# A mixture-of-experts layer computed by dispatch: token rows sorted by expert, scattered to tiles of 128 slots and gathered back

## The chip, the cores and the metric

The kernel runs on one core of one Trainium2 chip. The metric is the time of one execution on the device in microseconds (us). The profile is of one further execution, recorded by the hardware. The engines are TensorE (PE; its weight loads are listed as PEld), VectorE (DVE), ScalarE (ACT), GpSimd (POOL) and SyncE (SP, which here issues most DMAs). Each engine runs its own program in order, and they wait for each other by semaphores. The core's 16 DMA engines are shared by the queues of SP, ACT and POOL.

## The reference, cut to what matters

There are 2 sequences of 1024 tokens of 128 features, all float32. Layer 0 is a causal attention of 16 heads and then the mixture of experts that is changed; layer 1 is a recurrence (RWKV) of 4 inner layers and a small mixture of 8 experts. Layer 1 needs all of layer 0's output of a sequence. The changed part is, with T = 2048 tokens, 64 experts of width 64 and one shared expert of width 128:

```
shared = silu(x @ sg_w.T) * (x @ su_w.T) @ sd_w.T
scores = sigmoid(x @ gate_w.T) + gate_bias           # [T, 64]
mask   = the 4 best of 8 groups of 8 experts
topk_w, topk_i = top_k(scores * mask, 6);  topk_w /= topk_w.sum() + 1e-8
comb   = zeros(T, 64) with topk_w at topk_i
h      = silu(einsum('th,eih->eti', x, eg_w)) * einsum('th,eih->eti', x, eu_w)
routed = einsum('eti,ehi,te->th', h, ed_w, comb)
out    = shared + routed
```

Each token has 6 of the 64 experts. The einsum over all experts is 64/6 times the work that the chosen ones need.

## The kernel before

The kernel holds activations transposed, features on the 128 partitions and tokens along the free axis: `G.x` is 128 x 2048, cut into 4 chunks of 512 tokens (`CH`, `NC` = 4; a chunk is one bank of PSUM). `stage_front` loads, normalises and projects; `stage_core` has the attention and the first layer's experts; `stage_rwkv` has all of layer 1.

The attention runs in 8 groups (4 heads of one sequence each) of 24 units. Scores go through banks 0 to 3, ACT takes their exponential, POOL masks the diagonal blocks, and TensorE multiplies with the values. Beside the units TensorE also computes the row maxima of the next group ("fills", banks 4, 5 and 7); they come back as rows through small DMAs (`neg_rows`, L598). In the last group the output projection, layer norm, router logits and routing (DVE) of chunks 0 to 2 run beside the units (`beside`, `last_group`).

The experts are dense. Step 0 is the shared expert, and steps 1 to 32 take two experts each, side by side in 128 hidden rows; so 33 steps of 4 chunks, 132 turns. A turn is three float32 matmuls of 128x128 weights on 512 columns (`gate`, `up`, `down`; L861, L866, L871), a Silu on ACT, and two multiplications on DVE (L1240, L1248), the second by the token's weight for that expert, which SP brings as broadcast rows (`factors`, L610) from a table in DRAM. `down` adds into 4 banks of PSUM over all steps. The loop over steps is rolled from step 6 on. At its end DVE adds the 4 banks times a gate to `G.x` (L1312), and `stage_rwkv` begins.

The order of work on each engine is written out by hand: `prologue` interleaves chunk 3's attention output and routing with the first steps, and `steps` runs the rest. SP loads weights two steps ahead, each load behind a wait for the last reader of its tile.

## Time and profile before

| What | Value |
|---|---|
| Time, median of 2 runs | 1076.97 us (1076.29 to 1077.66) |
| Span of the profiled execution | 1085.5 us |
| Attention's last matmul ends | about 322 us into the span |
| Last `down` of the experts ends | about 678 us |
| PE busy | 1016.3 us, 94% of the span |
| DVE, ACT, POOL busy | 767.1, 562.5, 63.4 us |
| Mean granted TensorE clock | 0.976 of full |

The span runs from the profiled execution's first to its last instruction; it is the only time that is known of that execution, and it is 8.5 us (0.8%) above the median of the unprofiled runs. Times in the rows are us from the start of the span, except where a column says ns.

### The profile page before, as it was taken

How to read it: one execution, taken by the hardware profiler on the slowest of the kernel's cores; microseconds unless marked ns; L12 is line 12 of the kernel's file. 1: busy time of each engine (PE TensorE's matmuls, PEld its weight loads, DVE VectorE, ACT ScalarE, POOL GpSimd, SP SyncE). 2: the span in 40 equal slices, each digit the busy share in tenths (PEclk: the TensorE clock that was granted, in tenths of full speed). 3: DMA queues.
4: the chain of work that ended last, by engine and by line, in shares of the span. 5: the costliest groups of instructions: out<-in, count | busy, mean ns of one | idle time of the engine just before them, and what ended most of it. 6: DMA issues, size and time to landing. Idle time of an engine off the chain costs nothing. (4 is left out here: it accounts for less than half of the span.)

```text
span 1085.5 us, 12065 instructions
## 1 busy us (share of the span) xinstructions
PE 1016.3 (94%) x3707; PEld 434.1 (40%) x3707; DVE 767.1 (71%) x1331; ACT 562.5 (52%) x854; POOL 63.4 (6%) x152
## 2 busy tenths in 40 slices
PE   6889999999888999999999999879999999998998
PEld 3553334444333344444444444324334433443433
DVE  4878788888466755555555555488889888987675
ACT  3324566666775222222222222567788768875743
POOL 1011122222210000000000000000000000000000
PEclk9899899999999999999999999889999999998999
DMA  2732122210021355555554552200000020000001
GB/s 84 230 78 49 37 55 56 55 48 12 7 60 46 84 134 126 109 133 120 113 134 112 119 133 50 63 1 0 10 22 8 3 51 0 1 0 1 1 1 39
DMA packets 36571, 64.66 MB, mean 60 GB/s; under 512 B 8514, under 2 KB 27824, under 8 KB 31920
## 3 DMA queue, kind: packets, MB, share of 16 engines
...
## 5 line engine op out<-in xcount | busy, mean ns | idle before, releaser
L1083 DVE TENSOR_REDUCE part_max<-psum 128x1 f32<-128x512 f32 (+3 forms) x304 | 184.6, 657 | 37.3 <-PE psum L723 21.4
L948 ACT ACTIVATE pt<-psum 128x1024 f32<-128x1024 f32 (+1 forms) x192 | 150.0, 814 | 112.5 <-PE psum L741 112.1
L1240 DVE TENSOR_TENSOR moe_gu<-moe_silu,psum 128x512 f32<-128x512 f32 x132 | 90.6, 687 | 141.4 <-PE psum L866 137.1
L1069 ACT ACTIVATE moe_silu<-psum 128x512 f32<-128x512 f32 x112 | 66.9, 597 | 222.1 <-PE psum L861 222.1
L861 PE MATMUL psum<-h,moe_wt 128*128 128x512 f32 x264 | 135.8, 596 | 1.0 <-issue 1.0
L866 PE MATMUL psum<-h,moe_wt 128*128 128x512 f32 x264 | 135.4, 594 | 1.4 <-DVE moe_gu L1240 1.4
L871 PE MATMUL psum<-moe_hid,moe_wt 128*128 128x512 f32 x264 | 135.3, 594 | 1.0 <-DVE moe_hid L1248 1.0
L719 PE MATMUL psum<-ka,qa 72*128 72x512 bf16 (+3 forms) x384 | 115.8, 342 | 4.5 <-DVE part_max L1083 1.6
L741 PE MATMUL psum<-qa,ka 75*128 75x512 bf16 (+3 forms) x384 | 95.3, 331 | 4.0 <-DMA qa<-neg_t 2.3
L1248 DVE TENSOR_TENSOR moe_hid<-moe_gu,qa 128x512 f32<-128x512 f32 x120 | 83.1, 692 | 15.7 <-DVE moe_gu L1240 5.8
L757 PE MATMUL psum<-pt,va_g 128*32 128x512 f32 (+3 forms) x768 | 82.9, 504 | 0.5 <-POOL pt L690 0.3
L871 PEld LDWEIGHTS psum<-moe_hid,moe_wt 128*128 128x128 f32 x264 | 50.3, 191 | 65.4 <-issue 63.6
L866 PEld LDWEIGHTS psum<-h,moe_wt 128*128 128x128 f32 x264 | 49.7, 190 | 66.4 <-issue 56.4
L861 PEld LDWEIGHTS psum<-h,moe_wt 128*128 128x128 f32 x264 | 50.2, 191 | 63.5 <-issue 63.5
L719 PEld LDWEIGHTS psum<-ka,qa 72*128 72x128 bf16 x384 | 37.6, 99 | 80.0 <-DVE part_max L1083 58.9
L690 POOL TENSOR_SCALAR_AFFINE_SELECT pt<-pt 128x256 f32<-128x256 f32 x128 | 52.3, 410 | 219.0 <-ACT pt L948 218.3
L1570 PE MATMUL psum<-mix_c,wt_c 128*128 128x512 f32 x128 | 61.1, 600 | 0.0
L83 PE MATMUL psum<-ln_sq,mean 128*128 128x512 f32 x88 | 49.5, 658 | 11.4 <-ACT ln_sq L92 11.4
L1580 PE MATMUL psum<-kf,wt_c 128*128 128x512 f32 x128 | 57.9, 594 | 0.0
L1527 PE MATMUL psum<-hp,wt_a 128*128 128x512 f32 x96 | 50.0, 603 | 2.7 <-issue 2.7
L723 PE MATMUL psum<-mask_qk,identb 128*128 128x128 bf16 x256 | 50.5, 226 | 0.0
L1528 PE MATMUL psum<-hp,wt_a 128*128 128x512 f32 x96 | 49.8, 600 | 0.0
(264 smaller groups left out, 1301.6 us busy)
## 6 DMA issues: line engine op xcount, KB each, us to landing
...
qa<-rows_q SPq DMA_DIRECT2D x21, 192.0 KB
ka<-rows_k SPq DMA_DIRECT2D x21, 192.0 KB
...
wt_c<-in_channel_w SPq DMA_DIRECT2D x4, 576.0 KB, 4.0
...
```

The costliest lines, as they stand in the source:

```text
L719: mm = pe.matmul(bank[:, nk * h:nk * (h + 1)], qa[0:ROWS, g % RING, h0 + h, chunk(i, P)], ka[0:ROWS, g % RING, h0 + h, k0:k0 + nk], start= ...
L741: mm = pe.matmul(out[:, 0:n], ka[0:ROWS + 3, g % RING, 2 * p + k, chunk(j, P)], qa[0:ROWS + 3, g % RING, 2 * p + k, q0:q0 + n], start=True ...
L757: mm = pe.matmul(acc_bank[32 * h:32 * h + 32, q0 - CH * c:CH], va_g[k][:, j, h, :], pt[:, 2 * (q % 2) + h // 2, h % 2, 0:n], start=(j == 0 ...
L861: pe.matmul(gate_bank(n)[:, :], weights[:, 0, :], G.h[:, chunk(c)], start=True, stop=True).then_inc(g_psum, 1)
L866: pe.matmul(u_bank[:, :], weights[:, 1, :], G.h[:, chunk(c)], start=True, stop=True).then_inc(u_psum, 1)
L871: pe.matmul(y_bank[c][:, :], weights[:, 2, :], hid[:, at, :], start=first, stop=last, skip_group_check=True).then_inc(y_psum, 1)
L948: act.activation(pt[:, u % 4, :, 0:n], score_bank[u % 2][:, :, 0:n], ACT.Exp, scale=SCALE)\
L1069: act.activation(sg[:, c % 2, :], g_bank[:, :], ACT.Silu).then_inc(silu_done, 1)
L1083: dve.tensor_reduce(part_max[:, h0:h0 + heads, slot], bank_of("fill", f)[:, 0:heads * nk].rearrange("p (h n) -> p h n", h=heads), AX_X, AL ...
L1240: dve.tensor_tensor(gu[:, at % 2, :], sg[:, at % 2, :], u_bank[:, :], ALU.mult).then_inc(gu_done, 1)
L1248: dve.tensor_tensor(hid[:, at, :], gu[:, at % 2, :], tile[:, chunk(c)], ALU.mult).then_inc(hid_done, 1)
L1570: pe.matmul(G.bank[6 + j % 2][:, :], wt_c[u // 2 % 2][:, WCK + j, :], mix_c[:, 0, q, :], start=True, stop=True)\
```

## The change

The dense loop is replaced by dispatch.

- Routing also keeps, per token and expert, whether it is chosen (`picked`). `positions(b)` counts the tokens of each expert of a sequence with matmuls, rounds each count up to a multiple of 128, and gives every (token, choice) a row in a table of slots; a tile of 128 slots has one expert. There are always 112 tiles per sequence, in 28 quads of 4 (`QUADS`), 56 quads in all, whatever the counts are; the table of one sequence is 14336 rows of 512 bytes.
- ACT's queue fills both tables with zeros during attention groups 1 to 4 (8 DMAs of 1.8 MB). The chunks of `h` are turned to token rows by TensorE. POOL scatters: 48 indirect DMAs per sequence, each of 128 rows of 512 bytes.
- The shared expert runs for 4 chunks between the attention and the quads (`shared`, `shared_down`).
- A quad is loaded by SP (256 KB), turned by 4 transposes, multiplied by its tiles' gate and up weights (4 matmuls of 128 columns), turned again after Silu and product, multiplied by the down weights (4 more), copied by ACT, and stored by SP (256 KB). The weights of all experts lie in SBUF (6 MB, in 4 parts, loaded during the last attention groups); their offset is read from SBUF into registers of TensorE (`pe.load`).
- POOL gathers 6 rows for each token (48 indirect DMAs per sequence), DVE weights and adds them (`combine`), TensorE turns the sums back, and DVE adds them to `G.x`.
- Semaphores of the first stage are cleared and freed, and those of layer 1's experts are made earlier.

The diff, cut to its core; `link` makes DVE wait for the instruction before:

```diff
+def load_experts(sp, G, A, k, sem):
+    few = slice(16 * k, 16 * (k + 1))
+    sp.dma_start(G.qa[:, k, :, :].rearrange("p h t -> p (h t)").bitcast(F32), A["moe_gu"][:, few, :].rearrange("p e m -> p (e m)"))\
+        .then_inc(sem, 16)
+    sp.dma_start(G.ka[0:64, k, :, :].rearrange("p h t -> p (h t)").bitcast(F32), A["moe_d"][:, few, :].rearrange("p e m -> p (e m)"))\
+        .then_inc(sem, 16)
...
+    QUADS = -(-((TOP * S - E) // P + E) // 4)
...
+        xs = pt[:, 0:2, :, :].rearrange("p u k n -> p (u k) n")
+        ys = pt[:, 2:4, :, :].rearrange("p u k n -> p (u k) n")
...
+                def weights(k):
+                    sp.wait_ge(score_psum, NU * (NG - RING + k + 1))
+                    load_experts(sp, G, A, k, experts_in)
+                def load_quad(n):
+                    if n >= 4:
+                        sp.wait_ge(xs_psum, n - 3)
+                    sp.dma_start(xs[:, n % 4, :], xs_d[n // QUADS].rearrange("(q p k) m -> q p (k m)", p=P, k=4)[n % QUADS])\
+                        .then_inc(xs_in[n % 4], 16)
+                def store_quad(n):
+                    sp.wait_ge(y_kept, n + 1)
+                    sp.dma_start(ys_d[n // QUADS].rearrange("(q p k) m -> q p (k m)", p=P, k=4)[n % QUADS], ys[:, n % 4, :])\
+                        .then_inc(ys_out[n % 4], 16)
 
...
                     neg_rows(g + 2)
                 pack(LAST - 1, 1)
+                weights(2)
                 pack(LAST, 0)
...
-                with sp.Fori(PRE // 2, (STEPS - 3) // 2) as i:
-                    for k in (1, 0):
-                        s = 2 * i + 2 - k
-                        sp.wait_ge(u_psum, 4 * s + 4)
-                        load_expert(sp, A, s + 2, wt[k], slice(0, 2), gu_in[k])
-                        sp.wait_ge(hid_done, 4 * s + 4)
-                        factors(s + 2, factor[1 - k], slice(0, T), factor_in[1 - k])
-                        sp.wait_ge(y_psum, 4 * s + 4)
-                        load_expert(sp, A, s + 2, wt[k], slice(2, 3), down_in[k])
+                weights(3)
+                for b in range(B):
+                    sp.wait_ge(scattered[b], 16 * INDEXED)
+                    sp.wait_ge(pv_done, NQ * NG)
+                    for q in range(4):
+                        load_quad(QUADS * b + q)
+                    for q in range(QUADS):
+                        store_quad(QUADS * b + q)
+                        if q + 4 < QUADS:
+                            load_quad(QUADS * b + q + 4)
...
+                def scatter(b):
+                    pool.wait_ge(zeroed[b], 16 * ZERO_PARTS)
+                    pool.wait_ge(h_kept, 2 * b + 2)
+                    pool.wait_ge(row_done, b + 1)
+                    for n in range(BLOCKS * b, BLOCKS * (b + 1)):
+                        for j in range(TOP):
+                            pool.indirect_dma_start(out=xs_d[b], out_offset=bass.IndirectOffsetOnAxis(ap=row[:, n, j:j + 1], axis=0),
+                                                    in_=h_tok[:, n, :], in_offset=None).then_inc(scattered[b], 16)
+                def gather(b):
+                    for r in range(4):
+                        pool.wait_ge(ys_out[r], 16 * (QUADS // 4) * (b + 1))
+                    for n in range(BLOCKS * b, BLOCKS * (b + 1)):
+                        if n >= 4:
+                            pool.wait_ge(combined, n - 3)
+                        for j in range(TOP):
+                            pool.indirect_dma_start(out=yg[:, n % 4, j, :], out_offset=None, in_=ys_d[b],
+                                                    in_offset=bass.IndirectOffsetOnAxis(ap=row[:, n, j:j + 1], axis=0))\
+                                .then_inc(gathered[n % 4], 16)
...
+                for b in range(B):
+                    scatter(b)
+                for b in range(B):
+                    gather(b)
...
+                def positions(b):
+                    pe.wait_ge(picked_done, 2 * b + 2)
+                    pe.wait_ge(const_done, 4)
+                    pe.wait_ge(prob_done, NU * NG)
+                    tiles = range(BLOCKS * b, BLOCKS * (b + 1))
+                    for n in tiles:
+                        mm = pe.matmul(count_bank[b][:, 0:E], all_ones[:, :], picked[:, n, :], start=(n == tiles[0]),
+                                       stop=(n == tiles[-1]))
+                    mm.then_inc(count_psum, 1)
+                    pe.matmul(rank_bank[b][:, :], earlier[:, :], picked[:, tiles[0]:tiles[-1] + 1, :].rearrange("p n e -> p (n e)"),
+                              start=True, stop=False, skip_group_check=True)
+                    for k in range(BLOCKS - 1):
+                        mm = pe.matmul(rank_bank[b][:, E * (k + 1):CH], all_ones[:, :],
+                                       picked[:, tiles[k]:tiles[k] + 1, :].to_broadcast([P, BLOCKS - 1 - k, E]),
+                                       start=False, stop=(k == BLOCKS - 2), skip_group_check=True)
+                    mm.then_inc(rank_psum, 1)
...
+                def turn_rows(n):
+                    pe.wait_ge(xs_in[n % 4], 16 * (n // 4 + 1))
+                    if n >= 2:
+                        pe.wait_ge(xs_kept, n - 1)
+                    for k in range(4):
+                        mm = pe.transpose(xs_bank[n % 2][:, chunk(k, P)], xs[:, n % 4, chunk(k, P)], G.ident[:, :])
+                    mm.then_inc(xs_psum, 1)
...
+                def gates(n):
+                    ids = at_expert[n % 4]
+                    pe.load(ids, expert_at[0:1, n // QUADS, 4 * (n % QUADS):4 * (n % QUADS) + 4])
+                    held[n] = [pe.snap(x, min_val=0, max_val=(E - 1) * P) for x in ids]
+                    pe.wait_ge(xs_kept, n + 1)
+                    if n >= 2:
+                        pe.wait_ge(hid_done, n - 1)
+                    for k in range(4):
+                        mm = pe.matmul(gu_bank[n % 2][:, chunk(k, P)], xs_t[:, n % 2, chunk(k, P)], gu_w[:, bass.ds(held[n][k], P)],
+                                       start=True, stop=True)
+                    mm.then_inc(gu_psum, 1)
+                def turn_hidden(n):
+                    pe.wait_ge(hid_done, n + 1)
+                    if n >= 2:
+                        pe.wait_ge(hid_kept, n - 1)
+                    for k in range(4):
+                        mm = pe.transpose(hid_bank[n % 2][0:64, chunk(k, P)], hid[:, n % 2, k, :], G.ident[:, :])
+                    mm.then_inc(hid_psum, 1)
+                def downs(n):
+                    pe.wait_ge(hid_kept, n + 1)
+                    if n >= 2:
+                        pe.wait_ge(y_kept, n - 1)
+                    for k in range(4):
+                        mm = pe.matmul(y_bank[n % 2][:, chunk(k, P)], hid_t[:, n % 2, chunk(k, P)], down_w[:, bass.ds(held[n][k], P)],
+                                       start=True, stop=True)
+                    mm.then_inc(y_psum, 1)
+                def turn_combined(c):
+                    pe.wait_ge(combined, 4 * c + 4)
+                    for t in range(4):
+                        mm = pe.transpose(comb_bank[c][:, chunk(t, P)], h_tok[:, 4 * c + t, :], G.ident[:, :])
                     mm.then_inc(comb_psum, 1)
...
+                def after_attention():
+                    positions(0)
+                    turn_h(2)
+                    turn_experts(0)
...
                     for c in range(NC):
...
+                        shared(c)
+                        shared_down(c)
+                def experts():
...
+                    for b in range(B):
+                        for step in range(QUADS + 3):
+                            n = QUADS * b + step
+                            if step < QUADS:
+                                turn_rows(n)
+                            if 1 <= step <= QUADS:
+                                gates(n - 1)
+                            if 2 <= step <= QUADS + 1:
+                                turn_hidden(n - 2)
+                            if step >= 3:
+                                downs(n - 3)
...
-                prologue()
-                steps(pe, step)
+                after_attention()
+                experts()
+                pe.wait_ge(xs_kept, NQUADS)
+                for c in range(NC):
+                    turn_combined(c)
...
+                def clear(part):
+                    b, k = part // ZERO_PARTS, part % ZERO_PARTS
+                    n = QUADS // ZERO_PARTS
+                    if part == 0:
+                        act.wait_ge(const_done, 1)
+                    act.dma_start(xs_d[b].rearrange("(q p k) m -> p q (k m)", p=P, k=4)[:, n * k:n * (k + 1), :],
+                                  zero[:, :].unsqueeze(1).to_broadcast([P, n, CH])).then_inc(zeroed[b], 16)
 
...
+                def keep_rows(n):
+                    act.wait_ge(xs_psum, n + 1)
+                    if n >= 2:
+                        act.wait_ge(gu_psum, n - 1)
+                    act.copy(xs_t[:, n % 2, :], xs_bank[n % 2][:, :]).then_inc(xs_kept, 1)
+                def silu(n):
+                    act.wait_ge(gu_psum, n + 1)
+                    if n >= 2:
+                        act.wait_ge(hid_done, n - 1)
+                    act.activation(sg[:, n % 2, :, :], gu_bank[n % 2][:, :].rearrange("p (k m) -> p k m", k=4)[:, :, 0:64], ACT.Silu)\
+                        .then_inc(silu_done, 1)
+                def keep_y(n):
+                    act.wait_ge(y_psum, n + 1)
+                    if n >= 4:
+                        act.wait_ge(ys_out[n % 4], 16 * (n // 4))
+                    act.copy(ys[:, n % 4, :], y_bank[n % 2][:, :]).then_inc(y_kept, 1)
+                def experts():
+                    for b in range(B):
+                        for step in range(QUADS + 3):
+                            n = QUADS * b + step
+                            if step < QUADS:
+                                keep_rows(n)
+                            if 1 <= step <= QUADS:
+                                silu(n - 1)
+                            if step >= 3:
+                                keep_y(n - 3)
...
+                def positions(b):
+                    at = slice(BLOCKS * b, BLOCKS * (b + 1))
+                    dve.wait_ge(count_psum, b + 1)
+                    link(dve.tensor_scalar(rounded[:, 0, :], count_bank[b][:, 0:E], P - 1.0, None, ALU.add))
+                    link(dve.tensor_scalar(rounded[:, 1, :], rounded[:, 0, :], 7, 7, ALU.arith_shift_right, ALU.arith_shift_left))
+                    link(dve.tensor_copy(sizes[:, :], rounded[:, 1, :]))
...
+                    link(dve.scalar_tensor_tensor(before_row[:, :], ends[:, :], 1.0, sizes[:, :], ALU.add, ALU.subtract))
+                    dve.wait_ge(rank_psum, b + 1)
+                    ins = dve.tensor_tensor(key[:, b, :, :], rank_bank[b][:, :].rearrange("p (n e) -> p n e", n=BLOCKS),
+                                            before_row[:, :].unsqueeze(1).to_broadcast([P, BLOCKS, E]), ALU.add)
+                    ins.then_inc(rank_read, 1)
+                    dve.wait_ge(rank_read, b + 1)
+                    link(dve.tensor_tensor(key[:, b, :, :], key[:, b, :, :], picked[:, at, :], ALU.mult))
+                    for n in range(BLOCKS):
+                        last = dve.max(top_key[:, BLOCKS * b + n, :], key[:, b, n, :])
+                    link(last)
...
+                    dve.tensor_tensor(row[:, at, :], row_part[:, 0, :, :], row_part[:, 1, :, :], ALU.bitwise_or).then_inc(row_done, 1)
...
+                def slot_weights(n):
+                    link(dve.tensor_tensor(same[:, :, :], key[:, n // BLOCKS, n % BLOCKS, :].unsqueeze(1).to_broadcast([P, TOP, E]),
+                                           top_key[:, n, 0:TOP].unsqueeze(2).to_broadcast([P, TOP, E]), ALU.is_equal))
+                    link(dve.tensor_tensor(same[:, :, :], same[:, :, :], chosen[:, n, :].unsqueeze(1).to_broadcast([P, TOP, E]), ALU.mult))
+                    link(dve.tensor_reduce(weight[:, n, :], same[:, :, :], AX_X, ALU.add))
...
+                def hidden(n):
                     dve.wait_ge(silu_done, n + 1)
...
+                    if n >= 2:
+                        dve.wait_ge(hid_psum, n - 1)
+                    dve.tensor_tensor(hid[:, n % 2, :, :], sg[:, n % 2, :, :],
+                                      gu_bank[n % 2][:, :].rearrange("p (k m) -> p k m", k=4)[:, :, 64:P], ALU.mult).then_inc(hid_done, 1)
+                def keep_hidden(n):
...
+                    dve.tensor_copy(hid_t[:, n % 2, :], hid_bank[n % 2][0:64, :]).then_inc(hid_kept, 1)
...
+                def combine(n):
+                    r = n % 4
+                    dve.wait_ge(scattered[n // BLOCKS], 16 * INDEXED)
+                    dve.wait_ge(gathered[r], 16 * TOP * (n // 4 + 1))
+                    dve.tensor_tensor(yg[:, r, :, :], yg[:, r, :, :], weight[:, n, :].unsqueeze(2).to_broadcast([P, TOP, P]), ALU.mult)\
+                        .then_inc(weighted, 1)
+                    dve.wait_ge(weighted, n + 1)
+                    dve.tensor_reduce(h_tok[:, n, :], yg[:, r, :, :].rearrange("p j m -> p m j"), AX_X, ALU.add).then_inc(combined, 1)
+                def add_experts(c):
+                    dve.wait_ge(comb_psum, c + 1)
+                    dve.scalar_tensor_tensor(G.x[:, chunk(c)], comb_bank[c][:, :], G.mod[:, 0, 5, c // 2:c // 2 + 1],
+                                             G.x[:, chunk(c)], ALU.mult, ALU.add).then_inc(G.x_l0, 1)
...
+                def experts():
+                    for b in range(B):
+                        for step in range(1, QUADS + 2):
+                            n = QUADS * b + step
+                            if step <= QUADS:
+                                hidden(n - 1)
+                            if step >= 2:
+                                keep_hidden(n - 2)
+                            if b and step % 3 == 0 and 0 < step // 3 <= BLOCKS:
+                                combine(step // 3 - 1)
+                    for n in range(BLOCKS, NT):
+                        combine(n)
+                    for c in range(NC):
+                        add_experts(c)
```


## Rows read from the trace of the kernel before

**Rows 1.** The page: busy time by engine, and TensorE's and the DMA engines' slices.

```profile
PE 1016.3 (94%) x3707; PEld 434.1 (40%) x3707; DVE 767.1 (71%) x1331; ACT 562.5 (52%) x854; POOL 63.4 (6%) x152
...
PEclk9899899999999999999999999889999999998999
DMA  2732122210021355555554552200000020000001
```

**Rows 2.** Windows: the end of attention, and the expert stage.

```profile
core 0: us, PE busy (x) PEld busy (x) DVE busy (x) ACT busy (x) POOL busy (x), PEclk, DMA share, GB/s
278.00:322.00 44.00, 36.37 (x238) 13.52 (x237) 24.54 (x95) 30.99 (x49) 9.33 (x23) 1.00 0.16 37
323.00:677.00 354.00, 347.92 (x813) 152.86 (x814) 198.28 (x347) 93.85 (x149) 0.00 (x0) 1.00 0.47 109
```

**Rows 3.** The page's costliest groups: the three matmuls of the expert loop.

```profile
L861 PE MATMUL psum<-h,moe_wt 128*128 128x512 f32 x264 | 135.8, 596 | 1.0 <-issue 1.0
L866 PE MATMUL psum<-h,moe_wt 128*128 128x512 f32 x264 | 135.4, 594 | 1.4 <-DVE moe_gu L1240 1.4
L871 PE MATMUL psum<-moe_hid,moe_wt 128*128 128x512 f32 x264 | 135.3, 594 | 1.0 <-DVE moe_hid L1248 1.0
```

**Rows 4.** Groups of DVE by line and shape: by number of columns.

```profile
L1248 DVE TENSOR_TENSOR moe_hid<-moe_gu,qa 128x512 f32<-128x512 f32 x120 | 83.1, 692 | 15.7 <-DVE moe_gu L1240 5.8 <-DMA qa<-comb_rows 2.1
...
L2157 DVE TENSOR_TENSOR den<-e,bb 128x1024 f32<-128x1024 f32 x8 | 9.7, 1216 | 0.0
...
L1191 DVE MAX8 best<-wide 128x8 f32<-128x64 f32 x16 | 2.4, 214 | 0.1
...
L1166 DVE TENSOR_TENSOR score<-score,gate_bias 128x256 f32<-128x256 f32 x4 | 1.7, 425 | 0.1
```

**Rows 5.** The 8 KB copies qa<-neg_t (L598): issue time, and landing.

```profile
L598 SPq DMA_DIRECT2D qa<-neg_t x27: 516/590/791, 54.4 to 280.6; - x27
...
DMA to landing us min/median/max: 1.8/1.9/3.7
```

**Rows 6.** Groups of TensorE by line and shape: small f32 matmuls and transposes.

```profile
L1677 PE MATMUL psum<-ident,x 128*128 128x128 f32 x16 | 2.6, 286 | 0.9 <-DVE x L2260 0.8
L794 PE MATMUL psum<-ident,chosen 128*64 128x128 f32 x16 | 2.5, 276 | 2.5 <-DVE chosen L1212 1.5 <-DVE h L1146 1.1
```

**Rows 7.** TensorE in order of time: 128-column matmuls at either clock.

```profile
25.20 1.05 PE L364 MATMUL psum<-wqkv,h_attn 128*128 128x128 f32 x8
26.09 0.60 PE L342 MATMUL psum<-ident,x_tok 128*128 128x128 f32 x4
...
56.37 3.13 PE L120 MATMUL psum<-ident,centre 128*128 128x128 f32 x16
59.34 0.60 PE L741 MATMUL psum<-qa,ka 75*128 75x512 bf16 x2
```

**Rows 8.** ScalarE's groups: the copy of one bank of PSUM.

```profile
L955 ACT COPY acc<-psum 128x512 f32<-128x512 f32 x16 | 9.5, 592 | 1.8 <-PE psum L757 1.7
```

**Rows 9.** The kernel's last stores (L1490, 256 KB each): time of the issue itself.

```profile
L1490 SPq DMA_DIRECT2D out_x<-v_s x2: 372/372/372, 1078.2 to 1082.8; - x2
```

**Rows 10.** DMA issues by tile: operation, count, KB each, median us from issue to landing.

```profile
wt_c<-in_channel_w SPq DMA_DIRECT2D x4, 576.0 KB, 4.0
...
raw_a<-in_time_w SPq DMA_DIRECT2D x4, 192.0 KB, 2.3
...
out_x<-k_s SPq DMA_DIRECT2D x2, 256.0 KB, 2.3
```

**Rows 11.** A register operation of SyncE in the old loop (L610).

```profile
L610 SPq FUSED_REGOPS  x52: 51/51/66, 398.5 to 656.7; - x52
```

**Rows 12.** TensorE in order of time: after an idle gap, in layer 1.

```profile
700.52 2.02 PE L1527 MATMUL psum<-hp,wt_a 128*128 128x512 f32 x2 [2.71 <-issue]
702.34 1.84 PE L1528 MATMUL psum<-hp,wt_a 128*128 128x512 f32 x2
...
719.80 3.24 PE L75 MATMUL psum<-r,centre 128*128 128x512 f32 x4 [3.61 <-DVE r L1342]
```

437 lines of the change are left out of this document (200 added, 237 removed).

## The prediction, made before the changed kernel was seen to run

> **What bounds the kernel now.** I read the page first: TensorE is busy 94% of the span and holds its full clock in nearly every slice [rows 1]. The windows then say what kind of busy it is. From 323 to 677 us TensorE works 347.9 of 354 us at clock 1.00, while DVE needs 198 and ACT 94 [rows 2]. The groups name the work: three lines of 264 records, together 406.5 us of busy time of which neighbours overlap a little [rows 3]. The expert stage lasts from the attention's last matmul at about 322 us to the last `down` at about 678, so 355 us, and is a pure TensorE stage. Everything that replaces it has to fit into those 355 us, whatever it saves in multiplications.
>
> **The span and the median.** The sum is made on the profiled span of 1085.5 us; I add its difference to the median of 1077 without scaling (0.8% of it is below what I can estimate).
>
> **Part 1, from the attention's end to the first quad.** `positions(0)` is on the path: 16 short bf16 matmuls, about 1 us, then on DVE two passes of 512 columns at 0.69 us, 8 MAX8 at some 0.15 us each (4 lines of them in a row, 214 ns alone), and about 12 linked small operations at 0.2 to 0.25 us [rows 4]: together 6.5 us. Then POOL issues 48 indirect DMAs, one after the other. No row shows one. Below it is bounded by an ordinary issue of SP, 0.5 to 0.6 us, and above by twice the whole round trip of a small copy, 1.9 us [rows 5], because 128 addresses have to be worked out by software. I take 1.25, the middle between issue and round trip, since issues need not wait for landings; so 48 x 1.25 = 60 us, plus 1.9 for the last to land and 2.6 for the first load. That makes 71 us. DVE has a chain of its own beside it: two `positions` (13), two chunks of routing (2 x 8), the shared expert in lockstep with TensorE and ACT (4 chunks of two matmuls on the path, 0.85 each, a Silu of 0.6, 0.69 and 0.75 on DVE: 3.8 each, 15), `slot_weights` of 16 blocks, each three operations on 384 columns (between 425 ns for 256 and 692 for 512, so 0.56 each [rows 4], 27 us in all), chunk 3's output and norm (6): 77 us before it can serve `hidden(0)`. So the phase takes 75 us, and scatters below 1.25 us would not shorten it.
>
> The Trainium skill weighs in here (DMA: Bandwidth & Descriptors, Anatomy of one DMA): a DMA from GpSimd has a fixed cost of about 2 us, most of which is completion latency, while descriptor generation is small. By that page successive issues could overlap and 48 of them would be nearer to the lower bound, so that the gather at the end would be some 30 us shorter; its section Rules for kernel authors (many small transfers are mostly overhead, coalesce them) speaks against the change. No row here shows which.
>
> **Part 2, one step of the quad loop.** TensorE's work in a step is 4 transposes, 4 matmuls, 4 transposes, 4 matmuls. Four float32 matmuls of 128 columns take 0.89 us from start to next start (25.20 to 26.09), and 4 transposes 0.60 to 0.65 with their tail, 0.5 without [rows 6, 7]. So 0.5 + 0.9 + 0.5 + 0.9 and a tail of 0.2 = 3.0 us at full clock. If this were all, 56 steps would be 168 us against 355. ACT's three operations (at most 0.59 each [rows 8]) and DVE's two (0.43 and at most 0.69 [rows 4], plus a third of a `combine` of 1.9) stay below that.
>
> But read SP's order. `load_quad(q + 4)` stands behind `store_quad(q)` in SP's queue, and `store_quad(q)` waits for `y_kept` of quad q. Quad q's `downs` is the last thing that TensorE does in step q + 3, and the first thing of step q + 4 is `turn_rows(q + 4)`, which waits for that very load. TensorE runs in order, so `gates`, `turn_hidden` and `downs` of the older quads wait behind it. The four buffers are thus worth nothing after the first four steps: every step is a closed ring. Its other half, after TensorE's last matmul: ACT copies y, 0.59 us [rows 8] and 0.05 of signalling; SP issues the store, 0.37 [rows 9]; the load lands. A 192 KB load takes 2.3 us, 576 KB takes 4.0 [rows 10], 4.4 ns per KB, so 256 KB is 2.6 alone. The 256 KB store that is 0.37 us ahead on the same 16 engines adds up to 1.13 - 0.37 = 0.76 if the two move one after the other, and nothing if they overlap; I take 3.1, between 2.6 and 3.4. Sum of this half: 0.65 + 0.37 + 3.1 = 4.1 us.
>
> Two more terms. `pe.load` reads 4 registers from SBUF between `turn_rows` and `gates`, in TensorE's own order. The trace has only register arithmetic, 51 ns [rows 11], as a lower end, and the 1.9 us round trip of the smallest copy as an upper one; a read of memory without a DMA lies between, and I take 0.8. The Trainium skill (DMA: Bandwidth & Descriptors, Latency and other measured facts) gives a floor of about 600 ns for `tensor_load`; by that the step would be 0.2 us shorter. And the clock: after idle gaps of 2.71 and 3.61 us TensorE runs its next matmuls at half clock (two records in 2.02 us where 1.02 is usual), for some 3 us [rows 12]. Here each step begins after 4 us of idling, so most of its work is at 1.2 GHz. The same small matmuls cost 1.65 times as much there: 16 records begin 2.97 us before the next (56.37 to 59.34) against 0.89 for 8, 1.78 for 16 [rows 7]. Fully slow the step's 3.0 would be 5.0; I take 1.3 of the 2.0, since the clock can come back within the step.
>
> The ring is then 3.0 + 1.3 + 0.8 + 4.1 = 9.2 us. It is paid in steps 4 to 27 of each sequence: 48 x 9.2 = 442 us. The first four steps of a sequence (10 us, with the inner waits of a pipeline that fills) and its three draining steps (6.5) make 33 us for both; the second sequence's first load again stands behind a last store, 4 us. Part 2 is 479 us.
>
> **Part 3, the tail.** After the last `y_kept` the store takes 0.65 + 2.3 us, and only then POOL gathers sequence 1: 48 x 1.25 = 60 us, 1.9 to land, a last `combine` of two operations on 768 columns (between 0.69 for 512 and 1.22 for 1024 [rows 4]), 1.9, 0.6 for the turn, 3.0 for `add_experts`, which the kernel before had too (0 here): 67 us. Sequence 0's gather lies beside sequence 1's quads, where DVE is idle most of the ring.
>
> **Part 4, beside the attention.** 14.7 MB of zeros at roughly 230 GB/s (from the 4.4 ns per KB) are 64 us of DMA time in groups 1 to 4, and DMA is only a fifth busy there [rows 1]. The row of neg copies that each group waits for is issued 5 units after a clear began; it may land up to a few us late: 0 to 12 us, I take 2. ACT issues 8 DMAs, hidden since ACT waits for TensorE in each unit. Clearing 23 semaphores behind a barrier: 1 us (0 to 3). The weights, 6 MB, come in the last groups; the fourth part lands behind the 71 us of part 1, and would cost about 7 us without that cover.
>
> **Sum.** New stage 75 + 479 + 67 = 621 us for 355: +266, and +3 from part 4: 1085.5 becomes 1354, and the median 1077 becomes about 1346.
>
> **The rivals.** (a) The ring as said, but the indirect DMAs dominate: at 2.5 us each the first phase is 131 us and the gather 120, together +116: 1462. For it speaks that software works out 128 addresses per DMA and no row caps it; against, nothing but the middle I chose. (b) The clock stays at 1.2 GHz through every step: the ring is 9.9 us, +34: about 1380. The Trainium skill's page (TensorE: Matmul & The Clock Gate, HAM oscillation) describes a loop whose DMA wait returns in each turn and which then starts cold every time; by that rule the time would be this one, and the trace agrees at the gaps of [rows 12] as far as single gaps can. (c) Clock full and loads quick (ring 7.2, indirect DMAs at 1.0): 75 + 346 + 37 + 55 = 513, so +158: about 1238. (d) The other side: the ring doesn't close, because a load lands before TensorE comes to `turn_rows`. Then the loop is bound by TensorE at 3.0 to 3.8 us, 56 x 3.4 = 190 us, and with 75 + 67 and 12 for draining and refilling it is 344, about 1069; with indirect DMAs at 0.6 us the tail shrinks by 31 us, to 1038, faster by 3.6%. It decides where the ring falls below (355 - 3 - 75 - 67 - 37) / 48 = 3.6 us, and speaking against it is the order of two lines in SP's queue: the wait for y can't be passed. (e) The stage doesn't shrink in columns as it says: 224 tiles of 128 slots are run always, 28672 rows for 12288; but that is in the sum.
>
> **How the numbers follow.** My forecast, the closed ring at 8 to 10.4 us with indirect DMAs of 1 to 1.8 us, spans 1275 to 1420 and has 0.62 (rival b's time lies in it, with 0.15 of that). Rival (a) has 0.15, rival (c) 0.15, rival (d) 0.04, and 0.04 is for what I haven't seen. The predicted time is that of the likeliest case, 1346. The range takes in (c) and reaches into (a) to 2.5 us per indirect DMA; left out are (d), the unseen and the slower half of (a), 0.16 in all: 1225 to 1470. About 2% is what a measurement of this kernel tells from no change; (d) splits around it: faster 0.03, same 0.02, slower 0.95.
>
> **What the changed profile would show.** TensorE's groups should be small ones and its busy share after 322 us below one half; the wait that heads its list should be the DMA into `pt` (xs) before `turn_rows`; starts of `turn_rows` should be 9.2 us apart after the fourth of a sequence and 3 to 4 us apart before; the granted clock between 0.5 and 1.0 in these windows. POOL's issues should be 1.25 us apart, 48 in a row, before the first quad and after the last. I am wrong in the main if TensorE waits for ACT or DVE in the loop instead, if steps are under 7 us, or if the POOL phases are longer than the ring's surplus.

## The result: 1441 us for 1077, and the profile of the changed kernel

The changed kernel takes 1440.96 us (median of two, 1437.92 to 1444.00) against 1076.97: the ratio is 1.338, with a 95% interval of 1.331 to 1.346. The profiled execution has a span of 1442.3 us, 356.8 more than the one before. It lies in the range I gave (1225 to 1470) and 95 us above the value. The page has these lines where [rows 1] stood:

```profile
PE 988.3 (69%) x4332; PEld 545.2 (38%) x4333; DVE 729.9 (51%) x1323; ACT 564.6 (39%) x888; POOL 249.6 (17%) x348
...
PEclk9899999995565555555755556565599999999999
DMA  4526551221210111111222211111100000100000
```

TensorE's busy time is hardly less than before. It runs fewer columns, but many of them at half clock: read PEclk, which is 5 or 6 tenths in nearly all slices from the tenth to the 29th. The windows, cut at the phases, are the answer to [rows 2]:

```profile
core 0: us, PE busy (x) PEld busy (x) DVE busy (x) ACT busy (x) POOL busy (x), PEclk, DMA share, GB/s
323.00:343.00 20.00, 9.02 (x18) 3.92 (x18) 14.21 (x61) 4.17 (x6) 15.43 (x16) 0.51 0.21 65
343.00:389.00 46.00, 3.57 (x18) 2.04 (x19) 9.63 (x49) 0.00 (x0) 35.03 (x37) 0.50 0.18 63
389.00:442.00 53.00, 18.68 (x24) 5.91 (x22) 5.77 (x9) 2.39 (x4) 40.20 (x43) 0.63 0.16 61
442.00:471.00 29.00, 6.93 (x28) 5.88 (x28) 26.66 (x49) 2.32 (x5) 3.04 (x3) 0.50 0.03 10
471.00:700.00 229.00, 137.82 (x625) 118.69 (x626) 29.41 (x55) 39.21 (x76) 0.00 (x0) 0.58 0.17 57
...
719.00:744.00 25.00, 0.19 (x2) 0.00 (x0) 3.42 (x4) 1.55 (x3) 14.26 (x15) 0.51 0.20 60
744.00:965.00 221.00, 133.30 (x615) 114.94 (x616) 43.89 (x65) 38.82 (x75) 21.86 (x24) 0.58 0.19 65
969.00:1032.00 63.00, 1.11 (x4) 0.71 (x4) 18.32 (x16) 0.00 (x0) 45.43 (x48) 0.50 0.18 50
```

Read them, with the start of layer 1 from the rows in order of time, as a sum from 316 us, where `positions(0)` begins, to 1037, where layer 1 begins: 155 us to the first `hidden(0)` at 471, 233 for the first sequence's quads, 262 for the second's, 71 for the tail, 721 in all. I had 75, 479 for both sequences, and 67.

The two long quad windows have TensorE at clock 0.58, idle 40% of the time. The groups name the wait:

```profile
L909 PE MATMUL psum<-ident,pt 128*128 128x128 f32 x224 | 61.4, 430 | 211.4 <-DMA pt<-slot_x 207.6 <-issue 3.8
...
L734 POOL DMA_INDIRECT slot_x<-va,slot_row x96 | 93.9, 979 | 36.4 <-issue 29.0 <-DVE slot_row L1371 7.5
...
L745 POOL DMA_INDIRECT part<-slot_y,slot_row x96 | 91.3, 951 | 491.8 <-DMA slot_y<-pt 398.8 <-DVE va L1442 65.6 <-issue 27.4
```

L909 is `turn_rows`, and its wait is the DMA into the quad's tile. One turn of the ring in order of time (weight loads left out):

```profile
578.02 0.32 SPq L668 DMA_DIRECT2D slot_y<-pt  x1
578.38 0.43 SPq L663 DMA_DIRECT2D pt<-slot_x  x1
581.08 1.12 PE L909 MATMUL psum<-ident,pt 128*128 128x128 f32 x4 [3.71 <-DMA pt<-slot_x]
581.99 1.92 PE L923 MATMUL psum<-qa,xs_t 128*128 x8
...
583.70 1.06 PE L932 MATMUL psum<-ident,moe_hid 128*64 128x128 f32 x4
...
584.69 2.07 PE L940 MATMUL psum<-ka,moe_hid_t 64*128 x8
...
586.80 0.58 ACT L1192 COPY pt<-psum 128x512 f32<-128x512 f32 x1 [2.47 <-PE psum L940]
587.41 0.32 SPq L668 DMA_DIRECT2D slot_y<-pt  x1
587.77 0.43 SPq L663 DMA_DIRECT2D pt<-slot_x  x1
```

From store to store 9.39 us, of which the copy of y, the store's issue and the load are 3.8. This is the ring of the prediction. About one step in three is a shorter one, of 8.3 to 8.5 us: there the clock comes back before the step's end, and the same `downs` takes 1.16 us, as in this line from 10 us earlier:

```profile
576.22 1.16 PE L940 MATMUL psum<-ka,moe_hid_t 64*128 x8
```

What the prediction did not have is the length of the first phase, and the hole of 25 us at 719. In the first phase the rows of DVE (the second routing and the shared expert, beside the scatter) look like this:

```profile
359.42 0.29 DVE L1355 TENSOR_TENSOR_SCAN ends<-all_one,sizes 128x64 f32<-128x64 f32 x1
360.61 0.23 DVE L1356 SCALAR_TENSOR_TENSOR before_row<-ends,sizes 128x64 f32<-128x64 f32 x1 [0.90 <-DVE ends L1355]
371.91 0.69 DVE L1358 TENSOR_TENSOR slot_key<-psum,before_row 128x512 f32<-128x512 f32 x1 [11.08 <-remote]
...
402.74 0.69 DVE L1414 TENSOR_TENSOR o_den<-o_den,psum 128x512 f32<-128x512 f32 x1 [8.13 <-remote]
408.27 0.75 DVE L1418 SCALAR_TENSOR_TENSOR x<-psum,mod,x 128x512 f32<-128x512 f32 x1 [4.84 <-remote]
```

L1358 waits for TensorE's ranking matmuls, which ended at 357.5, and for L1356 on its own engine, which ended at 360.8; it starts at 371.9. L1356 waits only for the instruction before it on its own engine, and starts 0.9 us after it. Operations that wait for nothing, such as 8 MAX8 in a row, run at their usual pace. That speaks against slow work or a contended port: what seems late is the moment at which an engine sees what it waits for, and the profile often knows no releaser for it (`remote`, `issue`). The delays begin 20 us after GpSimd's first indirect DMA (322.75), and its last is at 444.4.

Who waits for whom matters. One chunk of the shared expert, from the same stretch:

```profile
405.35 1.91 PE L893 MATMUL psum<-h,shared_w 128*128 128x512 f32 x2
...
413.91 0.60 ACT L1173 ACTIVATE o_den<-psum 128x512 f32<-128x512 f32 x1 [16.24 <-remote]
418.88 0.69 DVE L1414 TENSOR_TENSOR o_den<-o_den,psum 128x512 f32<-128x512 f32 x1 [9.86 <-remote]
419.62 2.07 PE L902 MATMUL psum<-o_den,shared_w 128*128 128x512 f32 x2 [10.71 <-DVE o_den L1414]
```

ACT starts 6.7 us after the matmul whose result it takes, and DVE, which waits for ACT and for a second matmul (over at 408.9), 4.4 us after ACT's end. TensorE starts 0.05 us after DVE's end. So it is in all the rows of these stretches: the long delays stand before operations of ACT and DVE that wait for TensorE. TensorE behind DVE or ACT, SyncE behind ACT and DVE's `hidden` behind ACT's Silu start 0.02 to 0.14 us later, with few exceptions, the longest 1.3 us. Late instructions, rather than late signals, would fit this pattern less well, but no run tells the two apart.

### The profile page after: what moved, and what is told of

Read it like the earlier page. It is cut to its first block and busy times, and to the rows that moved or that the text cites. A ratio compares the mean times of both kernels' runs of the same rounds, so it can differ in the third digit from the quotient of the medians.

```text
span 1442.3 us, 13431 instructions
## 1 busy us (share of the span) xinstructions
PE 988.3 (69%) x4332; PEld 545.2 (38%) x4333; DVE 729.9 (51%) x1323; ACT 564.6 (39%) x888; POOL 249.6 (17%) x348
## 3 DMA queue, kind: packets, MB, share of 16 engines
q0 software_dynamic: 6144, 12.60, 2.6%
## 5 line engine op out<-in xcount | busy, mean ns | idle before, releaser
L909 PE MATMUL psum<-ident,pt 128*128 128x128 f32 x224 | 61.4, 430 | 211.4 <-DMA pt<-slot_x 207.6
L745 POOL DMA_INDIRECT part<-slot_y,slot_row x96 | 91.3, 951 | 491.8 <-DMA slot_y<-pt 398.8
L1179 ACT COPY xs_t<-psum 128x512 f32<-128x512 f32 x56 | 32.8, 585 | 257.0 <-PE psum L909 219.6
L909 PEld LDWEIGHTS psum<-ident,pt 128*128 128x128 f32 x224 | 40.4, 216 | 225.4 <-DMA pt<-slot_x 220.0
L923 PE MATMUL psum<-qa,xs_t 128*128 x448 | 107.4, 420 | 10.9 <-issue 9.6
L923 PEld LDWEIGHTS psum<-qa,xs_t 128*128 128x128 f32 x448 | 99.1, 325 | 14.1 <-issue 12.5
L734 POOL DMA_INDIRECT slot_x<-va,slot_row x96 | 93.9, 979 | 36.4 <-issue 29.0
L940 PE MATMUL psum<-ka,moe_hid_t 64*128 x448 | 93.2, 371 | 1.5 <-DVE moe_hid_t L1432 1.5
L940 PEld LDWEIGHTS psum<-ka,moe_hid_t 64*128 64x128 f32 x448 | 79.9, 266 | 19.4 <-issue 19.4
L932 PE MATMUL psum<-ident,moe_hid 128*64 128x128 f32 x224 | 54.8, 395 | 12.4 <-DVE moe_hid L1425 11.2
```

Source lines behind the costliest of these rows:

```text
L734: pool.indirect_dma_start(out=xs_d[b], out_offset=bass.IndirectOffsetOnAxis(ap=row[:, n, j:j + 1], axis=0), in_=h_tok[:, n, :], in_offset= ...
L745: pool.indirect_dma_start(out=yg[:, n % 4, j, :], out_offset=None, in_=ys_d[b], in_offset=bass.IndirectOffsetOnAxis(ap=row[:, n, j:j + 1], ...
L909: mm = pe.transpose(xs_bank[n % 2][:, chunk(k, P)], xs[:, n % 4, chunk(k, P)], G.ident[:, :])
L923: mm = pe.matmul(gu_bank[n % 2][:, chunk(k, P)], xs_t[:, n % 2, chunk(k, P)], gu_w[:, bass.ds(held[n][k], P)], start=True, stop=True)
L940: mm = pe.matmul(y_bank[n % 2][:, chunk(k, P)], hid_t[:, n % 2, chunk(k, P)], down_w[:, bass.ds(held[n][k], P)], start=True, stop=True)
```

## Experiments

Twelve kernels were run, beside the kernel before. Where no interval is given the time is that of a single execution. "First hidden tile" is the start of DVE's first `hidden`, at 470.9 us in the changed kernel. Line numbers shift by a few lines from kernel to kernel.

### Taking the store out of the load's way

```diff
                     for q in range(QUADS):
-                        store_quad(QUADS * b + q)
                         if q + 4 < QUADS:
                             load_quad(QUADS * b + q + 4)
+                        store_quad(QUADS * b + q)
```

> In SyncE's order each load of a quad goes ahead of the store that used to precede it, so the loads run one step further ahead. Theory (the ring of load and store sets the quad's time, 9.0 us of which the store's wait and the load's landing are 3.8): the wait for pt<-slot_x in front of L909 goes away, a step falls to the sum of TensorE's own instructions, 6.2 us if the clock stays at half (1.1 + 2.0 + 1.1 + 2.1) and about 3.3 if it comes back; over some 52 steps the kernel is 145 to 300 us faster than the changed kernel, 1140 to 1295 us. Rival (the step is bound by the chain through ACT and DVE, and the load only happens to end last): the wait changes its name and the step stays above 8 us, gain under 50 us.

Measured: 1203.06 us (1192 to 1216), ratio to the kernel before 1.115 (1.109 to 1.121). Two lines in one queue were worth 238 us, in the middle of what the ring theory gave. TensorE in order of time (of the longest of these executions):

```profile
561.18 0.66 PE L909 MATMUL psum<-ident,pt 128*128 128x128 f32 x4 [0.75 <-DMA pt<-slot_x]
561.95 1.15 PE L923 MATMUL psum<-qa,xs_t 128*128 x8
562.94 0.60 PE L932 MATMUL psum<-ident,moe_hid 128*64 128x128 f32 x4
563.47 1.16 PE L940 MATMUL psum<-ka,moe_hid_t 64*128 x8
564.56 0.65 PE L909 MATMUL psum<-ident,pt 128*128 128x128 f32 x4
```

Set them beside the ring above: from L909 to the end of L940 the same four groups take 3.4 us (561.18 to 564.56) for 5.7 (581.08 to 586.76), so the clock had come back. It falls again in places: other steps of this execution still begin with an L909 of 1.1 us for four transposes, after waits of about 2 us. The wait for the load fell from 207.6 to 33.8 us over the 56 quads. It is not zero: a load is still behind the store of one quad earlier. A later version, with the stores one more quad back, bears this out: there the waits for loads, but for those at the start of a sequence, are under 1 us together.

### What slows the other engines beside the scatter

Six kernels change only how GpSimd scatters. First, a wait for the landing after every fourth indirect DMA:

```diff
+                            if (TOP * (n - BLOCKS * b) + j + 1) % 4 == 0:
+                                pool.wait_ge(scattered[b], 16 * (TOP * (n - BLOCKS * b) + j + 1))
```

> GpSimd waits after every fourth indirect DMA of the scatter until these have landed. Theory A (the long waits of DVE, ACT and TensorE between 343 and 453 us come from a backlog of GpSimd's transfers that builds up when 96 are issued without a wait): the hops between engines fall back to under 0.3 us, the shared expert takes under 20 us instead of 54, and the first hidden tile, at 471 us, comes no later than that, although the scatter itself takes 24 x 1.5 to 2 us longer. Theory B (they come from GpSimd's issuing itself, whatever is in flight): the hops stay at 2 to 10 us, and since the scatter lasts longer the first hidden tile comes 20 to 40 us later, and the kernel at 1460 to 1480 us.

Measured: 1384.42 us, first hidden tile at 411.2. Making GpSimd wait made the kernel 57 us faster. The same line as L1414 above:

```profile
367.33 0.69 DVE L1416 TENSOR_TENSOR o_den<-o_den,psum 128x512 f32<-128x512 f32 x1 [1.86 <-PE psum L898]
369.24 0.75 DVE L1420 SCALAR_TENSOR_TENSOR x<-psum,mod,x 128x512 f32<-128x512 f32 x1 [1.22 <-PE psum L904]
371.02 0.69 DVE L1416 TENSOR_TENSOR o_den<-o_den,psum 128x512 f32<-128x512 f32 x1 [1.03 <-PE psum L898]
```

A chunk of the shared expert takes 3.7 us, for some 16 in the changed kernel. I first read this as a backlog of transfers. The next two tell a backlog from a pause. In one, GpSimd waits before the k-th for the landing of the (k-4)th, on four semaphores in turn, which bounds the number in flight and costs no time:

```diff
+                            k = TOP * (n - BLOCKS * b) + j
+                            if k >= 4:
+                                pool.wait_ge(scattered[b][k % 4], 16 * (k // 4))
```

> GpSimd waits before indirect DMA k of a scatter for the landing of k-4 (four semaphores in turn). Since one lands some 2 us after its issue and they are issued every 1.27 us, that landing is past and the wait costs GpSimd nothing: the pace stays at 1.27 us, and only the number in flight is bounded. Theory A1 (what harms is the number issued ahead of their landing): stalls go, as with the wait for every fourth, and the first hidden tile comes at 405 to 412 us; 1370 to 1390 us. Theory A2 (what helped in the run before was the pause of 1.5 us in which GpSimd issued nothing, at each fourth): the pause is gone here, the stalls stay, first hidden tile at 460 to 475 us, 1430 to 1445 us.

Measured: 1459.81 us; the first indirect DMA at 335.5 and the first hidden tile at 483.5, 148.0 us apart, as in the changed kernel (322.75 and 470.9: 148.2). The stalls are there to the same length (11.75 for 11.08 before L1358's counterpart). GpSimd's pace was the same too: the 48th starts 60.5 us after the first, for 60.6. So theory A1 falls: the number in flight is not it, and the pause was. (The time misses the 1430 to 1445 that I expected. Of the 19 us more than in the changed kernel 12.7 come from ahead of the scatter; I don't know why.)

> The wait for the landing comes after every 16th indirect DMA instead of every fourth. In the changed kernel the other engines were slow first after some 16 indirect DMAs (20 us). Theory (a backlog that needs 16 or so to build up, and empties in a pause of 1.5 us): hops stay short, and the scatter is 18 x 1.5 us shorter than with a wait for every fourth; first hidden tile at 405 to 412 us, 1370 to 1385 us. Rival (the share of time in which GpSimd issues decides): with pauses of 1.5 in 22 us the stalls come back almost wholly, 1420 to 1445 us.

Measured with the wait after every 16th: 1427.12 us; first hidden tile at 416.4. The time lies in the rival's range and the first hidden tile nearer to the theory's: the shared expert is nearly undisturbed (waits of L1414's counterpart 8.8 us in all, for 31.8), but later DVE stands idle 25.5 and 9.7 us in a row beside the second scatter, the first time behind a Silu of ACT that starts 17.5 us after its matmul. Pauses of 1.5 us in 22 only delay the trouble.

The pace is then what counts. Starts after a pause, in the kernel that waits after every fourth:

```profile
339.48 0.97 POOL L734 DMA_INDIRECT slot_x<-va,slot_row  x1 [1.56 <-DMA slot_x<-va,slot_row]
...
346.02 0.97 POOL L734 DMA_INDIRECT slot_x<-va,slot_row  x1 [1.55 <-DMA slot_x<-va,slot_row]
```

and in the one that waits after every 16th:

```profile
347.21 0.97 POOL L734 DMA_INDIRECT slot_x<-va,slot_row  x1 [1.55 <-DMA slot_x<-va,slot_row]
368.85 0.96 POOL L734 DMA_INDIRECT slot_x<-va,slot_row  x1 [1.55 <-issue]
```

That is 6.54 us for four, 1.63 each, and 21.64 for 16, 1.35 each. Stalls come at 1.27, come late at 1.35, and don't come in the shared expert at 1.63.

Is it the indirect form, or any DMA from GpSimd? This kernel sends the same 64 KB blocks to consecutive rows, so the experts get other rows:

```diff
-                            pool.indirect_dma_start(out=xs_d[b], out_offset=bass.IndirectOffsetOnAxis(ap=row[:, n, j:j + 1], axis=0),
-                                                    in_=h_tok[:, n, :], in_offset=None).then_inc(scattered[b], 16)
+                            at = P * (TOP * (n - BLOCKS * b) + j)
+                            pool.dma_start(xs_d[b][at:at + P, :], h_tok[:, n, :]).then_inc(scattered[b], 16)
```

> The scatter's 96 indirect DMAs are replaced by 96 plain DMAs from GpSimd of the same 64 KB each, to consecutive rows (the experts then get the wrong rows; the amount of work stays). Theory A (the stalls come with the indirect form, whose 128 descriptors GpSimd makes): plain ones take under 1.27 us each to issue and the other engines' hops are short; first hidden tile 40 to 80 us earlier, 1360 to 1400 us. Theory B (any DMA that GpSimd issues does it): the stalls stay and the time stays within 20 us of 1441.

Measured: 1384.33 us, first hidden tile at 405.5, shared expert undisturbed (waits of L1414 7.4 us in all). A plain DMA costs GpSimd 0.54 us, and 96 of them, twice as dense as the indirect ones, slow nobody: theory A, the indirect form. It is not the amount of traffic: the profile counts 6144 packets and 12.60 MB in GpSimd's queue in either kernel. The plain ones also write consecutive rows; that was not varied by itself. And is it the bytes? Here each scattered row is 128 bytes instead of 512, to a narrower view, so the tiles hold other data:

```diff
-                            pool.indirect_dma_start(out=xs_d[b], out_offset=bass.IndirectOffsetOnAxis(ap=row[:, n, j:j + 1], axis=0),
-                                                    in_=h_tok[:, n, :], in_offset=None).then_inc(scattered[b], 16)
+                            pool.indirect_dma_start(out=xs_d[b].rearrange('r (f m) -> (r f) m', m=32),
+                                                    out_offset=bass.IndirectOffsetOnAxis(ap=row[:, n, j:j + 1], axis=0),
+                                                    in_=h_tok[:, n, 0:32], in_offset=None).then_inc(scattered[b], 16)
```

> The changed kernel with a scatter of 128 bytes a row instead of 512 (the first 32 values of each token row, to a narrower view of the same buffer, so the tiles hold other data); number and pace of the indirect DMAs stay. Theory B1 (what piles up is per indirect DMA or per row: descriptors, their queue entries or completions): the pace stays at 1.27 us and the stalls stay, first hidden tile at 460 to 475 us, 1430 to 1450 us. Theory B2 (it is the bytes: 64 KB in 1.27 us, 52 GB/s in rows of 512 bytes): stalls mostly gone, first hidden tile at 405 to 415 us, 1375 to 1395 us.

Measured: 1439.52 us, first hidden tile at 468.4, a median of 971 ns per indirect DMA. A quarter of the bytes changes nothing: B1, the cost is per DMA or per row.

The last one holds the second scatter back until DVE has done the slot weights:

```diff
                     pool.wait_ge(row_done, b + 1)
+                    if b:
+                        pool.wait_ge(weights_done, 1)
```

> The second sequence's scatter waits until VectorE has done the slot weights. Theory (only while GpSimd issues indirect DMAs are the other engines slow): after the first scatter, at about 384 us, the shared expert takes 15 us instead of 54 and the slot weights 29, so the first hidden tile comes at about 430 instead of 471 us; then the second scatter runs beside the quads for 61 us, and slows them as the first gather does in the changed kernel (a hole of 25 us for 24 gathers), so half or all of the 40 us is given back; 1400 to 1445 us. Rival (the shared expert and the second routing are slow for another reason, of their own): the shared expert still takes 50 us with GpSimd silent, first hidden tile at 470 us, 1441 us or more.

Measured: 1462.62 us, first hidden tile at 439.2. The first scatter ends at 394; DVE's long waits end with one of 9.23 at 399, and from there the shared expert runs at 3.7 us a chunk. So the slowness is bound to the indirect DMAs and outlasts them by some 5 us. But the second scatter, now beside the quads (440 to 501), makes a hole of 40 us in them:

```profile
467.58 0.59 ACT L1195 COPY pt<-psum 128x512 f32<-128x512 f32 x1 [14.35 <-remote]
477.40 0.59 ACT L1182 COPY xs_t<-psum 128x512 f32<-128x512 f32 x1 [9.23 <-remote]
499.10 0.38 ACT L1188 ACTIVATE moe_silu<-psum 128x256 f32<-128x256 f32 x1 [21.11 <-remote]
```

The gain of 32 us was given back and more. I had expected at most all of it, 1400 to 1445 us; 10 of the 22 us above the changed kernel lie ahead of the first scatter, which starts at 332.7 here. The last of these three lines is the longest delay shown here: the matmul that ACT waits for had ended at 474.4, and ACT itself was free from 478.0. The stall moves to whatever runs beside the indirect DMAs.

### Putting the parts together

Loads first, a wait after each fourth scatter and after each third gather:

```diff
                                 .then_inc(gathered[n % 4], 16)
+                            if (j + 1) % 3 == 0:
+                                pool.wait_ge(gathered[n % 4], 16 * (TOP * (n // 4) + j + 1))
```

> Three changes together: SyncE's loads ahead of its stores, the scatter's wait after every fourth, and a wait after every third indirect DMA of the gather. If the gains of the first two are of different stages they add up: 1203 - 57 = 1146 us; the gather's waits remove the hole beside the second sequence's first quads (12 to 25 us) but lengthen the gather after the last quad from 60 to 60 + 16 x 1.5 = 84 us, so 1140 to 1160 us. If the ring of load and store had only hidden the stalls of the other sort, the sum is not reached: over 1175 us.

Measured: 1148.98 us, ratio 1.065 (1.059 to 1.071). The two gains add up (1146 expected), so ring and stalls are two costs, in two places. The third change, the gather's waits, was expected to take as much in one place as it gives in another. The next one moves the stores one quad further back and the weights beside the quads.

```diff
+                            if not b and step <= NT:
+                                slot_weights(step - 1)
...
+                        if q:
+                            store_quad(QUADS * b + q - 1)
```

> As the run before, with SyncE's stores one quad later still and the slot weights computed beside the first sequence's quads. Theory: the quads no longer wait for VectorE's 16 x 1.7 = 28 us of weights; they start when the first scatter and the shared expert are done, about 8 to 12 us earlier than 411 (the first scatter lands at about 404 us), and a step has no wait for pt<-slot_x in it at all and takes 3.1 to 3.5 us at full clock: 56 quads in 195 us; 1100 to 1130 us. It would be faster than the kernel before (1077 us) only if the quads took under 160 us, which TensorE's own 3.0 us each doesn't allow.

Measured: 1120.21 us, ratio 1.041 (1.035 to 1.047), within the expectation; the quads last 198 us from the first `hidden` (407.3) to the last (604.9).

```diff
-                            if (TOP * (n - BLOCKS * b) + j + 1) % 4 == 0:
+                            if (TOP * (n - BLOCKS * b) + j + 1) % 6 == 0:
...
-                            if (j + 1) % 3 == 0:
+                            if b == 0 and (j + 1) % 3 == 0:
```

> As the version with stores a quad later and the weights beside the quads, but the scatter waits after every sixth indirect DMA (a mean of 1.5 us each, between the pace of 1.27 at which the other engines stalled and 1.66 at which they did not), and the gather after the last quad has no waits (only GpSimd and VectorE work there). Theory: 16 x 1.5 = 24 us less in the tail and 4 x 1.5 = 6 us less ahead of the first quad, 1120 - 30 = 1090 us, 1080 to 1100. If a mean of 1.5 us each is still too fast, the shared expert takes over 25 us and the kernel stays above 1105.

Measured: 1100.49 us, ratio 1.0185 (1.015 to 1.022; the kernel before took 1080.9 us on the chip of this run), 20 us better instead of 30. Whether this is slower than the kernel before by more than 2% is open. The tail gave its part, but the quads went from 198 to 217 us (405.0 to 622.2): beside them the second scatter now ran at 1.52 us each (326.52 to 335.62 for six, in the first scatter). That pace left the shared expert alone and still cost the quads: ACT's waits marked `remote` beside the second scatter come to 36 us here, up to 5.3 each, and to 19 us, up to 4.0 each, in the version with a wait after every fourth.

```diff
-                        for j in range(TOP):
+                        for j in range(TOP if b else 2):
                             pool.indirect_dma_start(out=xs_d[b], out_offset=bass.IndirectOffsetOnAxis(ap=row[:, n, j:j + 1], axis=0),
...
-                        for j in range(TOP):
+                        for j in range(1 if b else TOP):
                             pool.indirect_dma_start(out=yg[:, n % 4, j, :], out_offset=None, in_=ys_d[b],
```

> The version of the run before with indirect DMAs left out: in the first sequence only each token's first two picks are scattered (16 instead of 48), in the second only the first pick's result is gathered (8 instead of 48). The tiles, their matmuls, loads and stores stay. Theory (GpSimd's pace of 1.27 us for one indirect DMA bounds both ends): 32 x 1.5 = 48 us less ahead of the first quad, unless the second routing and the shared expert, done at about 377 us, take its place (then 25 us less), and 40 x 1.26 = 50 us less in the tail: 1090 - 75 to 98, 990 to 1015 us, under the kernel before. Rival (something else ends there last, VectorE's combining or the routing): under 40 us less.

This kernel leaves out part of the layer's result, to find a price. The first scatter, now of 16, has no waits in it. Measured: 1036.7 us, 64 less, and not the 75 to 98 that I expected. The first hidden tile came 20.7 us earlier (384.3), now behind the shared expert; the time from the start of the last sequence's gather to layer 1 fell from 68.2 to 24.3 us, where DVE's 8 combines of 2.4 us are the end. So 68 us of the profiled span (1103.4 to 1035.0) hang on the number of indirect DMAs, and with these left out the tiled experts beat the kernel before, in the one execution that there is.

```diff
+                            k = TOP * (n - BLOCKS * b) + j + 1
+                            if k % (3 if b else 6) == 0 and (b or k <= 36):
+                                pool.wait_ge(scattered[b], 16 * k)
...
-                    for n in range(NT):
+                    for n in range(12):
                         slot_weights(n)
...
+                            if not b and 8 <= step < 12:
+                                slot_weights(step + 4)
```

> The best version so far (1100 us) with the same work placed otherwise: twelve of the sixteen slot weights go back ahead of the quads, where VectorE was idle from 378 to 405 us while the first scatter ended; the first scatter's waits after each sixth stop at the 36th; the second scatter, which runs beside the first sequence's quads and is needed only some 100 us later, waits after every third. Theory (the quads, 4.0 us each against the 3.4 that TensorE's own instructions take at full clock, lose the rest to VectorE's extra work and to the slow hops beside the indirect DMAs): 5 to 15 us less in the quads and 1 to 2 ahead of them, 1083 to 1095 us. Rival (the loss is the same load and store ring, or the clock after each start): no change, 1096 to 1105 us. Neither theory brings it clearly under the kernel before.

Measured, as the median of 12: 1082.35 us (1074.4 to 1086.4) beside 1076.9 for the kernel before on the same chip, ratio 1.0042 (1.0012 to 1.0072): 0.4% slower, no difference by the bound of 2%. It is 18 us under the 1100.49 of the version with waits after every sixth, of which some 4 are the other chip (1080.9 there for the kernel before), and just under the range that I expected. Its windows show the quads at clock 0.91:

```profile
378.00:403.00 25.00, 4.73 (x27) 4.43 (x28) 17.96 (x33) 2.08 (x4) 17.38 (x17) 0.53 0.32 105
403.00:590.00 187.00, 171.20 (x1260) 151.75 (x1260) 79.36 (x134) 79.83 (x158) 92.79 (x92) 0.91 0.53 175
```

and ACT's copies of y are 3.0 us apart in long stretches of the first sequence:

```profile
439.68 0.58 ACT L1199 COPY pt<-psum 128x512 f32<-128x512 f32 x1 [0.57 <-PE psum L947]
...
442.68 0.59 ACT L1199 COPY pt<-psum 128x512 f32<-128x512 f32 x1 [1.14 <-PE psum L947]
...
445.68 0.58 ACT L1199 COPY pt<-psum 128x512 f32<-128x512 f32 x1
```

DVE is busy now in the window in which it used to wait, and the quads take 191.5 us from first to last `hidden` (402.5 to 594.0), for 217. None of ACT's waits beside the second scatter is marked `remote` any more. How much of the 25 us came from the gentler second scatter and how much from the weights was not separated.

## Why the prediction was right, and where its sum was off

**The bound.** That the stage was pure TensorE work of 355 us is what its rows show, and the new one is bound by none of the engines: in the quad windows even TensorE is busy only 60% of the time, while it waits for loads.

**Part 2, the ring.** Right in mechanism and, with some luck, in size. I gave 9.2 us a step; in the first sequence steps are 8.3 to 9.6 us apart, 9.1 in the mean of 24 (the one shown is 587.41 - 578.02 = 9.39). By its terms: TensorE's 3.0 at full clock is what the last version shows; the other half, 4.1, measured 3.7 to 3.8, since the load landed 2.7 after its issue and not 3.1, so the store ahead of it took next to nothing; `pe.load`, 0.8, measured nothing, as `gates` begins 0.9 us after `turn_rows` with no gap; the clock term of 1.3 was too small: TensorE's half of the ring is 5.6 us in the step shown where 3.0 would be full clock, so 2.6, and some 2.3 in the mean with the shorter steps. The misses (-0.3, -0.8, +1.0 in the mean) nearly cancel; that the sum is right to 0.1 us is luck. Swapping two lines confirmed it from the other side. Part 2 in all came to 495 us for 479, and the 16 more are the hole of 25 us during the first gather, less what the ring was shorter.

**Rival (b)**, the clock at its lower level through each step, holds for two steps in three: from 581.08 to 586.80 us the granted clock is 0.50. In the third it comes back on the way (0.64 from 490.69 to 495.40), and the step is a microsecond shorter. This rival gave 9.9 us a step; with `pe.load` at nothing it would be 9.1, also near the measured mean. The loop that the Trainium skill describes (TensorE: Matmul & The Clock Gate, HAM oscillation), cold at the start of every turn, is seen here: the four transposes after each load take 1.1 us, for 0.6 at full clock.

**Part 1, the first phase.** This is the step that failed: "75 us", and that DVE's chain of 77 us and GpSimd's 71 lie beside each other at no cost to either (75 is also less than the longer of the two). Each alone was well sized. GpSimd's part, from 316 us to the issue of the first quad's load at 385.6 and 2.7 for its landing, took 72. 1.25 us for an indirect DMA: measured 0.97 and a gap of 0.30, 1.27. `positions(0)`: 5.0 us for 6.5. `slot_weights`: 29 for 27. But between 343 and 453 us the hand-overs to ACT and DVE came late, one by 11 us after all that it waited for on its own engine and 14 after TensorE (357.5 to 371.9 above), the shared expert took 54 us for 15, and the phase 155. I had asked what an issue costs GpSimd and what it keeps from starting, not what it does to engines that share nothing with it. The price of that was 60 to 65 us in this phase (first hidden tile at 411.2 with waits, 405.5 with plain DMAs) and about 25 in the hole. The other 15 to 20 of the 80 are small misses: undisturbed, the shared expert ends at 377 and the weights at 405, so DVE's chain is 85 us and not 77, and the first hidden tile lies some 5 us into what I counted as the quads' filling.

**Part 3.** 67 us predicted, 71 measured; 48 gathers at 1.257 us. The lower bound for an indirect DMA, successive issues that overlap, didn't come: GpSimd is busy 0.95 to 0.97 us in each row of L734 and L745, and the next starts 0.30 later. By the Trainium skill (DMA: Bandwidth & Descriptors, Anatomy of one DMA) descriptor generation is small beside the fixed cost of some 2 us. Here GpSimd's own part, 1.26 us each one after the other, is the whole price of a row of 48; the rows don't say what share of it is descriptor generation. The rule of the Trainium skill to coalesce small transfers (DMA: Bandwidth & Descriptors, Rules for kernel authors) was the right warning: with 72 of the 192 left out, and the work with them, the kernel was 64 us faster.

**Part 4.** I had +3. The stage began no later than before (316 for 322), so no cost of the zeros is seen, though nothing here separates them from the other changes, and no run shows the 1 us for the semaphores. The stage took 721 us for the 621 that I had, but the span is only 88 above my 1354: 6 us for the earlier start and 3 for this part; most of the rest is that I count the stage to layer 1 here, 2.5 us past the end that the 355 us had.

**Rivals (a), (c), (d), (e).** (a) had the right place (the indirect DMAs) and the wrong mechanism: the issue wasn't 2.5 us, but its side effect brought the time near to this rival's (1441 for 1462), which is chance. (c) fell with the clock. (d) is the world of the first experiment: the ring opened, and the kernel was still not faster, because the phase ahead carried 80 us more than I had put in for it, and the quads took 264 us from the first `hidden` to the last where I had 190 for all of them. (e) was in the sum.
